# The first cross attention of a two-layer decoder, reordered by score bank and turned chunk

## The reference

```python
q = (x @ W_q).reshape(Bq, T1_, N_HEAD, D_HEAD).transpose(0, 2, 1, 3)
k = (context @ W_k).reshape(Bq, T2_, N_HEAD, D_HEAD).transpose(0, 2, 1, 3)
v = (context @ W_v).reshape(Bq, T2_, N_HEAD, D_HEAD).transpose(0, 2, 1, 3)
scores = jnp.einsum('bhqd,bhkd->bhqk', q, k) * atten_scale
scores = scores + bias[None, None, :, :] * head_scale[None, :, None, None]
attn = jax.nn.softmax(scores, axis=-1)
out = jnp.einsum('bhqk,bhkd->bqhd', attn, v).reshape(Bq, T1_, N_HEAD * D_HEAD)
return out @ W_out + b_out
```

## Time and profile before

| | us |
|---|---|
| median of 3 runs | 1626.83 |
| the runs | 1617.98 to 1628.32 |
| the profiled execution | 1618.68 |
| its span, first to last instruction | 1616.9 |

### The profile page before, as it was taken

One profiled execution on the slowest core, in us unless ns is written; L12 is line 12 of the kernel. 1 busy time (PEld: TensorE's weight loads), 2 busy tenths in 40 slices (PEclk: granted clock), 3 DMA queues, 4 the chain that ended last, 5 costly groups with the idle time before them and its releaser, 6 DMA issues.

```text
span 1616.9 us, 27253 instructions
## 1 busy us (share of the span) xinstructions
PE 1465.5 (91%) x9386; PEld 1068.1 (66%) x9386; DVE 1152.5 (71%) x2175; ACT 921.8 (57%) x1927; POOL 768.3 (48%) x424
## 2 busy tenths in 40 slices
PE   7878999999999999999997997789999999996798
PEld 4547777777777777877756964355555555553497
DVE  5457788778887777778726866567777777771687
ACT  3436666666566666666625754346666666664376
POOL 4134333323333333331103619048888888889353
PEclk9999999999999999999999999799999999998899
DMA  3131111110011111110021202154545454420110
GB/s 77 32 103 39 39 39 39 39 38 18 25 34 38 38 38 38 38 38 19 3 75 34 64 22 56 31 142 107 124 107 125 106 125 106 107 58 1 53 40 25
DMA packets 61042, 92.13 MB, mean 57 GB/s; under 512 B 9166, under 2 KB 47502, under 8 KB 60814
## 3 DMA queue, kind: packets, MB, share of 16 engines
q1 hardware_dynamic: 59566, 90.59, 21.9%
q10 hardware_dynamic: 1376, 0.26, 0.1%
HBM read 51.89 MB, written 1.97 MB: 33 GB/s over the span
## 4 chain that ended last, share of the span: by engine, by line
PE 66%; DVE 20%; issue 5%; ACT 4%; POOL 3%; SPq 1%; DMA 0%; ACTq 0%; POOLq 0%; DVEq 0%
PE PS L694 7%; DVE prob_a L1120 6%; PE PS L1304 6%; PE PS L1318 5%; PE PS L1284 4%; DVE HL L1138 3%; PE PS L710 3%; PE PS L1249 3%; PE PS L712 3%; PE PS L1621 3%; PE PS L711 3%; PE PS L1622 3%; PE PS L1623 3%; POOL QO_area L1407 3%; PE PS L671 2%
## 5 line engine op out<-in xcount | busy, mean ns | idle before, releaser
L1407 POOL TENSOR_TENSOR QO_area<-QO_area,prob_a 125x896 f32<-125x896 f32 x160 | 336.1, 2101 | 25.0 <-ACT prob_a L1492 3.6
L1138 DVE TENSOR_TENSOR HL<-PS,HL 125x512 fp32r<-125x512 f32 (+1 forms) x384 | 238.1, 623 | 139.4 <-ACT HL L1003 136.7
L1003 ACT ACTIVATE HL<-PS 125x512 fp32r<-125x512 f32 (+1 forms) x384 | 205.0, 534 | 175.8 <-PE PS L694 175.8
L1556 DVE TENSOR_REDUCE QO_area<-PS 112x1 f32<-112x500 f32 x384 | 239.0, 671 | 67.3 <-PE PS L1284 67.1
L866 POOL TENSOR_TENSOR HL<-ctx_area,ones 125x512 fp32r<-125x512 f32 (+1 forms) x64 | 94.4, 1475 | 360.3 <-PE PS L712 279.1
L1492 ACT ACTIVATE prob_a<-PS 125x448 f32<-125x448 f32 x384 | 187.6, 540 | 107.1 <-PE PS L1304 101.1
L1018 ACT ACTIVATE prob_a<-prob_a,neg_max 128x500 f32<-128x500 f32 x192 | 135.8, 707 | 85.8 <-DVE neg_max L1128 85.8
L710 PE MATMUL PS<-HL 125*128 125x512 f32 (+1 forms) x384 | 172.7, 450 | 0.2 <-DVE HL L1138 0.2
L1304 PEld LDWEIGHTS PS<-HL 98*125 98x125 f32 x768 | 102.4, 185 | 72.5 <-ACT prob_a L1492 40.1
L1284 PE MATMUL PS<-HL 96*112 96x500 f32 x384 | 131.6, 421 | 20.1 <-DVE QO_area L1556 11.7
L1304 PE MATMUL PS<-HL 98*125 98x256 f32 x768 | 144.2, 309 | 2.2 <-ACT prob_a L1492 2.2
(11 more groups left out here) (211 smaller groups left out, 3045.8 us busy)
## 6 DMA issues: line engine op xcount, KB each, us to landing
HL<-prob_b SPq DMA_DIRECT2D x128, 187.5 KB, 4.0
ctx_area<-in_ctx_T SPq DMA_DIRECT2D x16, 750.0 KB, 11.7
ctx_area<-in_ctx SPq DMA_DIRECT2D x16, 750.0 KB
HL<-ctx_area SPq DMA_DIRECT2D x64, 187.5 KB, 3.9
inv_area<-in_ctx_T SPq DMA_DIRECT2D x8, 750.0 KB, 4.2
prob_a<-in_ctx_T SPq DMA_DIRECT2D x8, 750.0 KB, 4.2
ctx_area<-in_L_ffn_w SPq DMA_DIRECT2D x16, 256.0 KB, 3.0
ctx_area<-in_L_ffn_W SPq DMA_DIRECT2D x16, 256.0 KB, 3.0
```

Of the source, the lines that this page charges most:

```text
L1003: nc.scalar.activation(pH[k % 3][0:KC, 0:n], PS[0:KC, 3 + k % 2, 0:n], ACT.Copy)\
L1138: nc.vector.tensor_tensor(pL[k % 3][0:KC, 0:n], PS[0:KC, 3 + k % 2, 0:n], pH[k % 3][0:KC, 0:n].bitcast(fp32), ALU.subtract)\
L1407: nc.gpsimd.tensor_tensor(late_acc[b % 2], before, late_p[n % LATE_P], ALU.add).then_inc(m["padd"], 1)
L1556: nc.vector.tensor_reduce(late_part[b % 2][:, u // NKB, u % NKB:u % NKB + 1], PS[0:2 * S, u % NKB, 0:KB], AX, ALU.max).then_inc(m["mx"], 1)
```

## The change

The stage is written anew for its one layer (the branches for another layer go), with these differences:

- PE alternates by unit. A batch has two phases of twelve steps. In phase (b, 1) the chunks are those of group 1 of batch b-1, and the units are 0 to 11 of batch b; in phase (b, 0) the chunks are group 0 of batch b, the units 12 to 20. The first three units of a phase stand ahead of its steps, with the last two products of the phase before between them. A step is: transposes of chunk k, a score unit if there is one, the product of chunk k-2.
- Score units use banks 0 and 1 by turns, each waiting for DVE to have taken the unit two before (`biased`); turned chunks use banks 2, 3, 4, and wait for `trc` of three before.
- DVE takes one unit and one chunk a step in place of three units and three or four chunks a slot; ACT one chunk and one exponential.
- The reciprocals (128 rows by 4 or 3) are transposed by PE (`turn_sums`, one transpose), copied by ACT, and spread by 4 or 3 matmuls of 128 columns (`spread_sums`). The diagonal on DVE and the matmul with ones go.
- The queries' low half moves from DVE to POOL, whose copy of the high half becomes a multiplication with ones, as for the keys. DVE's scaling waits for `q` besides.
- All engines' streams are written out; no hardware loop is left in this stage.

```diff
 def cross_tensor(pe, n):
-            def scores(b, par, s, j):
-                dst = PS[0:TROWS[l], j, 0:KB]
-                wait_past(pe, m["mx"], tiles * b + s, 1)
+            def score(b, u):
+                at = UNITS * b + u
+                if at >= 2:
+                    pe.wait_ge(m["biased"], at - 1)
+                dst = PS[:, at % 2, 0:KB]
...
             def transposes(b, g, k):
-                    wait_past(pe, m["trc"], at, 2)
-                    mm = nc.tensor.transpose(PS[0:KC, 3 + k % 2, j * n:(j + 1) * n],
+                if at >= 3:
+                    pe.wait_ge(m["trc"], at - 2)
+                    mm = nc.tensor.transpose(PS[0:KC, 2 + k % 3, j * 128:(j + 1) * 128],
...
-            def sums(b, g):
-                    mm = nc.tensor.matmul(PS[:, 7, 0:128 * size], ones[:, :],
-                                          inv_diag[g][:, 0:size, :].rearrange("p a b -> p (a b)"),
+            def turn_sums(b, g):
+                pe.wait_ge(m["inv"], at + 1)
+                nc.tensor.transpose(PS[0:SIZES[g], 7, 0:128], row_inv[:, GA * g:GA * g + SIZES[g]], ident[:, :])\
+            def spread_sums(b, g):
+                pe.wait_ge(m["turned"], 2 * b + g + 1)
+                for t in range(size):
+                    mm = nc.tensor.matmul(PS[:, 7, t * 128:(t + 1) * 128],
+                                          ident[0:size, t:t + 1].broadcast_to([size, 128]),
+                                          inv_rows[g][0:size, :], start=True, stop=True)
...
+            def phase(b, g):
+                mine = b - g
+                before = (b - 1, 1 - g) if b else None
+                for i in range(3):
+                    if b < B:
+                        score(b, (1 - g) * NKB * GA + i)
+                    if before and i < 2:
+                        product(*before, NC - 2 + i)
+                for k in range(NC):
+                    if mine >= 0:
+                        transposes(mine, g, k)
+                    if b < B:
+                        for u in score_units(g, k):
+                            score(b, u)
+                    if mine >= 0:
+                        if k >= 2:
+                            product(mine, g, k - 2)
+                        if k == 4:
+                            turn_sums(mine, g)
+                        if k == 6:
+                            spread_sums(mine, g)
+        def score_units(g, k):
+            if g == 1:
+                return (3 + k,) if k < 9 else ()
+            return (15 + 2 * (k // 3) + k % 3,) if k < 9 and k % 3 < 2 else ()
 def cross_gpsimd(pool):
-                    nc.gpsimd.tensor_copy(qH[par], QO_flat[:, bass.ds(b * HQ, HQ)]).then_inc(m["qh"], 1)
+                halve(qH[b % 2], qL[b % 2], QO[:, b, :], m["q"])
 def cross_vector(dve, chain):
+            def scale_out(b, g):
+                dve.wait_ge(m["q"], min(b + 2, B))
...
+            def phase(b, g):
+                if b < B:
+                    for i in range(3):
+                        add_bias(b, (1 - g) * NKB * GA + i)
+                for k in range(NC):
+                    if b < B:
+                        for u in score_units(g, k):
+                            add_bias(b, u)
+                    if mine >= 0:
+                        low_chunk(mine, g, k)
+                    if before and k == 1:
+                        scale_out(*before)
+                    if mine >= 0 and k == 2:
+                        reciprocals(mine, g)
```

More of the change, by code:

```diff
@@ L262, in decoder_kernel @@
         fold_mm, fold_ev, vo_out = sem("fold_mm"), sem("fold_ev"), sem("vo_out")
-        names = "q scores mx exp tr trc pv idiag inv invc norm out qh trh kspl vspl qp qpa qpd".split()
-        xa = [{n: sem(f"xa0_{n}") for n in names}]
+        names = ("q qp qpa qpd kspl vspl scores biased mx exp tr trh trc pv inv turn turned spread invc norm out").split()
+        xa0 = {n: sem(f"xa0_{n}") for n in names}
         ld_k = [sem("ld_k0")]
@@ L817, in cross_tensor @@
-            batch(0, 0)
-            batch(1, 1)
-            batch(2, 0)
-            with pe.Fori(3, B - 2, 2) as i:
-                batch(i, 1)
-                batch(i + 1, 0)
-            batch(B - 1, 1)
-            for k in range(NC):
-                transposes(B - 1, 1, k)
-                products(B - 1, 1, 1, k, False)
-            product(B - 1, 1, 1, NC - 2)
-            product(B - 1, 1, 1, NC - 1)
-            sums(B - 1, 1)
-            if l == 1:
-                pe.wait_ge(m["wo"], 1)
+                if k == 0 and b:
+                    pe.wait_ge(m["norm"], 2 * b + g - 1)
@@ new lines, in cross_tensor @@
+            pe.wait_ge(xn_ready, 2 * n + 2)
+            pe.wait_ge(fold_ev, 8)
+            for h in range(NH):
+                p = h % 2
+                if h >= 2:
+                    pe.wait_ge(m["qpa" if p == 0 else "qpd"], h // 2)
+                for a in range(2):
+                    mm = nc.tensor.matmul(PS[:, 2 * p + a, 0:HALF], qk_fold[:, h, :],
+                                          XN[:, a * HALF:(a + 1) * HALF], start=True, stop=True)
+                mm.then_inc(m["qp"], 1)
@@ L933, in cross_gpsimd @@
[L933 to L957 removed]
+            keys(0)
@@ L1178, in scale_out @@
                 ins.then_inc(m["norm"], 1)
-            def chunk(b, g, k, first):
-                copy_chunk(b, g, k)
-                if k == 2 and not first:
-                    scale_out(*((b, 0) if g else (b - 1, 1)))
-                if k == (9 if l == 0 else NC - 1):
-                    reciprocals(b, g)
-            def queries(b, par, part):
-                dve.wait_ge(m["qh"], b + 1)
-                n = HQ // 2
-                c = slice(part * n, part * n + n)
-                nc.vector.tensor_tensor(qL[par][:, c], QO_flat[:, bass.ds(b * HQ + part * n, n)],
-                                        qH[par][:, c].bitcast(fp32), ALU.subtract).then_inc(m["q"], 1)
@@ L1195, in batch @@
-            def batch(b, par):
-                first = isinstance(b, int) and b == 0
-                last = isinstance(b, int) and b == B - 1
-                for s in range(tiles):
-                    maxima(b, s)
-                    g, ks = slot_chunks(l, s)
-                    for k in ks:
-                        if g == 0:
-                            chunk(b, 0, k, first)
-                        elif not first:
-                            chunk(b - 1, 1, k, False)
-                    if l == 0 and s in (1, 2) and not last:
-                        queries(b + 1, 1 - par, s - 1)
-                    if l == 1 and not last and 3 < s < 7:
-                        values(b + 1, 1 - par, s - 4)
@@ L1224, in cross_vector @@
+            for b in range(B):
+                phase(b, 1)
+                phase(b, 0)
+            phase(B, 1)
             scale_out(B - 1, 1)
```

670 lines of the change are left out of this document (206 added, 464 removed).

## The result

| | before | changed |
|---|---|---|
| median, us | 1626.88 | 1577.38 |
| the runs | 1617.98 to 1628.32 (4) | 1573.78 to 1580.49 (4) |
| the profiled execution | 1618.68 | 1580.49 |
| its span | 1616.9 | 1578.4 |

The ratio is 0.9706, with a 95% interval of 0.9666 to 0.9747: faster by 2.5 to 3.3%. Of the changed kernel's four runs the profiled one is the slowest, and that of before lies near the bottom of its range. So the two medians differ by 49.5 us and the two profiled executions by 38.2.

The account below looks back on a forecast made before the run. PE was taken as the bound, idle 4.1 to 4.2 us a batch on DVE's subtraction. Gains of 53.4, 3.9 and 1.5, together 58.8 us, off 1618.7 give 1560, put at 1562 for scatter; range 1549 to 1594.

Parts of the forecast that it names:

- What bound the kernel: Batches of the stage: PE stands idle 4.1 to 4.2 us each, its transposes waiting for DVE's subtraction behind a tile's three units.
- A batch stays at 40.1 to 40.2: PE's own work: two transposes and seven 128-column matmuls, 2.0 us, replace two matmuls with ones, 1.9 us a batch.
- The idle allowance of 0.4 us a batch: PE's waits at steps 1 and 2, where DVE also scales and takes reciprocals: 0.4 us, making 40.5 us a batch.
- DVE's load: DVE's 34.4 us a batch loses the diagonal (2.76 us) and two query subtractions, ending near 30 of 40.
- The queries on POOL: Query splits on POOL take under 4.4 us a batch, covered by nearly a whole batch's lead; adds nothing.
- the written-out streams: PE loses its loop in this stage: between a gain of 4.2 us and a loss of as much, taken as 0.
- The first batch: Start of the stage: the first product moves from 129.89 to near 126, limited by POOL's splits; 3.9 us gained.
- The sum: 15 batches fall from 660.9 to 607.5 us, gain 53.4; with 3.9 at the start and 1.5 at the end, 58.8.
- Half-waits: DVE's backlog stays or alternating costs PE about 0.04 us at 45 places; batches 42.2, 1585 us (1578 to 1603); chance 0.15.
- the change doesn't do what it says: DVE takes in-order steps exactly following PE's, so PE merely waits at other places; 1603 to 1635 us; chance 0.06.
- DVE's place makes it slower: Phase (b, 0) from step 1: DVE's subtraction, behind the unit, falls two steps behind; batch 46.1, 1644 us; chance 0.04.
- the clock falls: PE at the 1.2 GHz level for a tenth of the stage: 4 us more a batch, about 1619 us; chance 0.03.

Follow-up runs that it names:

- old: The kernel before the change, 1626.88 us; the 44.3 us a batch is that kernel with its hardware loops written out, 1621.76 us, ratio 0.9992.
- reliefs alone: The kernel before, written out, with turned reciprocals and the queries' low half on POOL, its order and banks kept: 1603.7 us, ratio 0.989.
- reliefs and order, old banks: The changed kernel with three banks for scores and two for turned chunks, instead of two and three: 1597.44 us, ratio 0.9838.
- new: The changed kernel as described under the change, against the kernel before: 1577.38 us, ratio 0.9706.
- order and banks alone, no reliefs: The changed kernel with the diagonal and matmul with ones restored and the queries' low half back on DVE: 1571.45 us, ratio 0.9667.
- the doubled spread: The changed kernel with each spreading matmul of the reciprocals issued twice: 1623.62 us, ratio 1.0005.
- the version with the diagonal: The changed kernel with only the reciprocals taken back to the diagonal on DVE and the matmul with ones: 1561.72 us, ratio 0.9632.
- two and two: The changed kernel with two banks for turned chunks instead of three, and two for scores as changed: 1595.97 us, ratio 0.9836.

## Why the forecast held, and where its sizes were off

The forecast was 1562 us with 1549 to 1594; the median is 1577.38. The direction and the range were right, and so was the wait that would go; how much of it is the order's and how much the third bank's was not argued. The miss of 15 us is one step for the most part.

**What bound the kernel: right as to the wait, half right as to its cause.** PE's 4.1 to 4.2 us of idle time per batch were put down to DVE's tile-wise order, with two banks named beside it. In the experiments the period goes 44.3 (old), 42.95 (reliefs alone), 42.60 (reliefs and order, old banks), 41.29 (with the third bank, new) and 40.75 (order and banks alone, no reliefs), and the waits for the subtraction go with it. So the order needs its bank, and on this path the bank is the larger step.

**"A batch stays at 40.1 to 40.2": the step that failed.** I took the two transposes and seven spreading matmuls at 2.0 us against 1.9 for the two matmuls with ones. Both sizes were off. The rows of new say otherwise for the first (PE in order of time around the group 1 spread):

```profile
402.60 0.34 PE L654 MATMUL PS<-HL 125*128 125x384 f32 x1
402.87 0.93 PE L668 MATMUL PS<-inv_area,ident 3*128 3x128 f32 x6
403.72 0.59 PE L638 MATMUL PS<-ident,prob_b 128*125 128x128 f32 x3
404.07 0.47 PE L626 MATMUL PS<-HL 128*128 128x500 f32 x1
...
405.37 0.49 PE L638 MATMUL PS<-ident,prob_b 128*125 128x128 f32 x3
405.62 0.47 PE L626 MATMUL PS<-HL 128*128 128x500 f32 x1
```

The last product gives way after 0.27 us instead of 0.18, the six instructions take 0.85, and the three transposes behind them 0.35 instead of 0.25. From 402.60 + 0.18 to 403.72 + 0.10 that is 1.04 us, for group 0 in the same way 423.23 - 422.90 - 0.23 + 1.08 + 0.10 = 1.28, and the two turns take 0.11 each (420.06 to 420.17 for one): 2.5 us. The price of 0.116 an instruction from the earlier trace rows was right: in the doubled spread 16 of them take 1.98 us and in new 8 take 1.08, so one more costs 0.11. What I left out are the ends of a short burst. Each has 0.18 us more in itself, 0.1 ahead of it and 0.1 behind it, 0.37 in all and twice a batch; the turns were cheaper by 0.2 than my "at most".

The matmuls with ones, on the other side, are 1.5 us and not 1.9. The 1.08 us that I read at 415.50 held a part of the very wait that I was pricing separately: the weight load of the transposes behind waited there for the subtraction that DVE began at 415.97. Behind 768.80 the next start comes after 0.86 us (at 769.66), behind the smaller ones after 0.65, and the version with the diagonal has the same. So a packed batch of old is 39.7 us, its idle time about 4.5, and the exchange cost PE 1.0 us a batch where I had 0.1.

The forecast added 38.2 for steps and units, 2.0 for these small matmuls and 0.4 of allowance (40.6, which I had as 40.5); the small matmuls measured 2.5, and 0.5 took the place of the allowance. Taken back on the chip, the period fell by 0.8 and not 1.0, since 0.24 went into a new wait of a score. 15 x 0.8 is 12 us, which is what the ratios say; of the 15.7 of the medians, 3.4 is that the kernel before, too, was slower beside the change (1626.88 against 1623.45).

**The idle allowance of 0.4 us a batch: right in size, for another reason.** Steps and units, 13.6 + 10.3 + 14.3 = 38.2 us by my prices, take 41.29 - 2.54 = 38.75 in new: 0.5 more, where I allowed 0.4. But the allowance rested on DVE's backlog at steps 1 and 2, and the profile shows PE busy throughout. It is spent as dearer instructions instead, such as a product that stands directly behind transposes:

```profile
415.07 0.60 PE L638 MATMUL PS<-ident,prob_a 128*125 128x128 f32 x4
415.65 0.47 PE L652 MATMUL PS<-HL 125*128 125x512 f32 x1
...
416.42 0.60 PE L638 MATMUL PS<-ident,prob_a 128*125 128x128 f32 x4
416.78 0.47 PE L626 MATMUL PS<-HL 128*128 128x500 f32 x1
```

Here the product starts 0.58 us behind the transposes where the score starts 0.36 behind: a wait of 0.2 for the subtraction under the weight load, in 17 places. With the old reciprocals the period is 40.5, which is my forecast to the tenth, and that is luck: the ones were 0.4 cheaper than I had them and the rest as much dearer than I allowed.

**DVE's load: half right.** I expected some 30 of 40 us a batch, and it is 32.84 in 43, or 31.5 of 41.3. I counted the diagonal's 2.76 us as DVE's work; 2.07 of them were POOL's lock, which the new order would have removed without moving the reciprocals at all. This is the deeper cause of the failed step: the change paid with 0.8 us of PE, the bound, for 1.25 us of DVE (0.69 + 0.56), which has a quarter of its time free.

**The queries on POOL, and the written-out streams, at nothing: right** within what the times can tell, by 1578.63 against 1577.38 and by the ratio 0.9992; by the period the queries' move gains 0.24 us a batch.

**The banks: right for new, and not argued.** My working gave the margins of products and scores and said nothing of why the transposes need a third bank. They do, by 18.6 us, and my first expectation on that was wrong. The forecast of the whole gain leaned on a bank that its working didn't mention, and there it was lucky.

**The first batch: 3.9 us forecast, 1.0 found.** The first product comes 3.3 us earlier (129.89 to 126.59), but 2.3 of that were won ahead of the stage: POOL's first query step starts at 104.05 us instead of 106.36. That start moves by as much between kernels that differ only in the use of banks (104.65 with two and two, 106.61 with three for scores), so it is not the change's. I had made POOL's splits the limit. PE and DVE in order of time show another:

```profile
115.89 0.50 PE L626 MATMUL PS<-HL 128*128 128x500 f32 x1
...
116.87 0.74 DVE L884 CUSTOM_DVE_ANT_0 prob_a<-PS,proj_w,head_scale 128x500 f32<-128x500 f32 x1 [0.19 <-PE PS L628]
...
117.67 0.50 PE L626 MATMUL PS<-HL 128*128 128x500 f32 x1
```

With nothing but scores to issue, two units take 117.67 - 115.89 = 1.78 us, 0.89 each and not the 0.73 of DVE alone: with two banks a unit waits until DVE has taken the unit two before, so that PE's 0.9 and DVE's 0.7 stand in a ring. With a third score bank (the experiment above) they come every 0.68, and then the transposes wait for ACT's exponentials (L828):

```profile
121.61 0.39 PE L626 MATMUL PS<-HL 128*128 128x500 f32 x1
...
122.29 0.39 PE L626 MATMUL PS<-HL 128*128 128x500 f32 x1
...
124.55 0.70 PE L638 MATMUL PS<-ident,prob_a 128*125 128x128 f32 x4 [1.42 <-ACT prob_a L828]
```

So the ring held the scores back, and behind it stands ACT: of what the third bank saved on the scores, the first product got 1.5 us.

**The sum, again.** From the first product to the output projection it is 692.4 us before and 648.9 after: 43.4 gained where 53.4 + 1.5 = 54.9 were forecast; 15 batches at 0.79 too much are 11.9 of the missing 11.5. What the two ends of the stage gave together is 1.9 us, 1.5 forecast for the last; the spread stands at another place within a batch than the matmul with ones did, so that the ends can't be read singly.

**The rivals.** Half-waits gave 1585, nearer in time than the forecast by half, but for a reason that isn't there: no wait for the subtraction worth its name remains. Its other arm, 0.04 us for each alternation, would be 1.8 us a batch, and steps and units together are only 0.5 above their prices. That the change doesn't do what it says, that DVE's place makes it slower, and that the clock falls in new are refuted by the period and by 1.00. The sentence that small transposes between other work might cost more than a row of before shows named the right kind of error, at other instructions: the spreading matmuls.

## What to carry to other kernels

When the bound is one engine's idle time, order the waiting engine's work by the unit in which it is waited for, and walk every wait on the buffers between them, not only that of the last consumer: here the order and one PSUM bank together gave everything, and on the path that was run the bank was the larger part. Work moved onto the bound in order to relieve an engine with room is paid in full; price it by a burst of its own length and with its two ends, and read the price of what it replaces at more than one place. And before an instruction's long duration is counted as work, look at what the other engine does at that moment, and at the same instruction in other batches: four times the duration of its like was a lock and not a load.

## What the runs showed of the hardware

- A DVE pass with two SBUF inputs, 128x512, took 2.76 us with a POOL multiplication beside it and 0.69 us alone, and ended 0.54 us after POOL. In the kernel before it took 0.69 in 6 of 16 batches. The profile counts the blocked time as busy.
- PE's clock fell to 0.50 for about 3 us behind 16 small fp32 matmuls (4 partitions by 128 columns) with no idle time ahead, from the fourth doubled batch on, and that cost 1.6 us a batch; behind 8 of them it stayed at 1.00. The cause is not shown.
- Eight fp32 instructions of 4 partitions by 128 columns took 1.08 us from their start to the next, 16 took 1.98: 0.11 each, as 24 in a row of full height (0.116), and 0.18 once. What stood just before and just behind such a burst took 0.1 us more each.
- The first matmul behind transposes takes 0.31 us to the next start, the same behind another matmul 0.23 (128x500).
- Four hardware loops more or less: 0.9992 (0.9972 to 1.0013).
